# One scan per two channel blocks in a Mamba and mixture-of-experts layer on one core

## The reference, cut to what matters

```python
xc, z = split(layernorm(x) @ in_proj_w.T, 2)
u  = causal_conv(xc, conv_w) + conv_b        # 4 taps, all channels mixed
dt = clip(sigmoid(u @ dt_w.T + dt_b), 1e-4, 1)
A  = -exp(A_log);  B = u @ B_w.T;  C = u @ C_w.T
for each token t:                            # state: 512 channels x 16
    dA    = exp(clip(dt[t] * A, -5, 5))
    state = dA * state + dt[t] * B[t] * u[t] + 1e-6
    y[t]  = sum_n(state * C[t]) + D * u[t]
x = x + (y * silu(z)) @ out_w.T
```

## Time and profile before

| | us |
|---|---|
| median of three runs | 3082.39 |
| profiled execution | 3076.53 |
| its span, first to last instruction | 3074.5 |
| first scan starts | 87.0 |
| first down product of a tile starts | 2418.2 |

### The profile page before, as it was taken

The page is one execution under the profiler, slowest core; times in us unless marked ns, Lnnn a source line. Parts: engine busy times, 40 slices in busy tenths (PEclk is TensorE's granted clock), DMA queues, the critical chain, the costliest instruction groups (busy, mean ns, idle before and its releaser), DMA issues. The chain is left out here.

```text
span 3074.5 us, 57196 instructions
## 1 busy us (share of the span) xinstructions
PE 2651.9 (86%) x15616; PEld 2307.9 (75%) x15616; DVE 2131.7 (69%) x4576; ACT 2115.1 (69%) x4987; POOL 2462.9 (80%) x1667
## 2 busy tenths in 40 slices
PE   6788888898888888988988888889876699999997
PEld 4677877787777777877877777788765577777776
DVE  1889889889888998899899888998894111111111
ACT  1878888888887888888888887888783233333332
POOL 1989999989998999999899988999993365656555
PEclk9889989989988899899898898898987899999999
DMA  3222222223222222222222222222220677777775
GB/s 134 99 70 80 80 73 80 74 75 97 81 77 75 89 73 85 77 74 81 74 79 98 75 76 74 89 74 87 70 70 21 171 184 180 184 177 185 178 184 126
DMA packets 136253, 309.91 MB, mean 101 GB/s; under 512 B 14992, under 2 KB 79632, under 8 KB 135696
## 3 DMA queue, kind: packets, MB, share of 16 engines
q1 hardware_dynamic: 108880, 270.03, 28.0%
q0 software_dynamic: 27072, 36.46, 6.1%
HBM read 258.42 MB, written 48.01 MB: 100 GB/s over the span
## 5 line engine op out<-in xcount | busy, mean ns | idle before, releaser
L1023 POOL TENSOR_TENSOR room<-dtu,b_all 128x1024 f32<-128x1024 f32 x512 | 1202.8, 2368 | 13.3 <-POOL dtu L1000 5.9
L809 ACT ACTIVATE bank<-room,eps_col 128x512 f32<-128x512 f32 x1024 | 693.8, 684 | 309.2 <-DVE carry L1261 213.2
L796 ACT ACTIVATE room<-room,neg_a 128x256 f32<-128x256 f32 x2048 | 868.5, 499 | 9.6 <-DVE room L1247 7.6
L604 PE MATMUL bank<-ident,room 128*128 128x128 f32 x4096 | 556.7, 293 | 239.2 <-DVE room L1256 201.3
L604 PEld LDWEIGHTS bank<-ident,room 128*128 128x128 f32 x4096 | 501.7, 152 | 293.5 <-DVE room L1256 219.5
L1247 DVE TENSOR_TENSOR_SCAN bank<-room,carry,bank 128x256 f32<-128x256 f32 x864 | 580.9, 736 | 61.6 <-ACT bank L809 52.7
L1012 POOL TENSOR_TENSOR room<-room,c_all 128x1024 f32<-128x1024 f32 x224 | 531.8, 2374 | 112.6 <-ACT carry L814 69.2
L1327 DVE SCALAR_TENSOR_TENSOR hid<-hid,bank 128x256 f32<-128x256 f32 (+1 forms) x312 | 131.0, 420 | 631.9 <-ACT up L905 631.9
L1247 DVE TENSOR_TENSOR_SCAN room<-room,carry,bank 128x256 f32<-128x256 f32 x672 | 448.4, 726 | 12.2 <-ACT bank L809 11.5
L1163 POOL DMA_INDIRECT out<-room,ids x144 | 227.7, 1581 | 251.2 <-ACT room L986 221.4
L559 PE MATMUL bank<-xnT,w_conv 128*128 128x256 f32 x3072 | 404.2, 288 | 2.2 <-ACT xnT L832 2.2
(11 more groups left out here) (150 smaller groups left out, 3294.6 us busy)
## 6 DMA issues: line engine op xcount, KB each, us to landing
b_all<-b_scratch SPq DMA_DIRECT2D x128, 512.0 KB, 4.0
c_all<-b_scratch SPq DMA_DIRECT2D x128, 512.0 KB, 5.8
room<-in_wgu SPq DMA_DIRECT2D x72, 704.0 KB, 4.8
room<-in_wd SPq DMA_DIRECT2D x72, 384.0 KB
room<-x_by_expert SPq DMA_DIRECT2D x72, 260.0 KB, 2.7
x_in<-in_x SPq DMA_DIRECT2D x32, 256.0 KB, 5.4
x<-in_x SPq DMA_DIRECT2D x32, 256.0 KB, 2.6
out<-x SPq DMA_DIRECT2D x32, 256.0 KB, 4.2
```

The lines of the kernel that those rows point to most:

```text
L604: last = mm(tr_bank[k][:, b * P:(b + 1) * P], v[n % VRING][:, b, k * P:(k + 1) * P], ident[:, :], is_transpose=True, start=False, stop=(n ...
L796: last = af(da[n % RING][:, b, :], dt[c.par][:, b, :], ACT.Exp, scale=neg_a[:, b, n:n + 1])
L809: af(v_slot(n, h)[:, :], v[n % VRING][:, 2 * h:2 * h + 2, :].rearrange("p b t -> p (b t)"), ACT.Identity, bias=eps_col[:, 0:1]).then_inc(v ...
L1023: nc.gpsimd.tensor_tensor(out=v[n % VRING][:, :, :], in0=dtu[:, :, :], in1=row, op=ALU.mult) \
```

## The change

- The first column of each decay block stays 0 (written once), ScalarE writes columns 1 to 255, and one scan of 512 columns goes over two blocks with the initial value 0.0.
- What the state before brings to a block's first column (decay of the first token x carry) is added to the first column of dt x u x B before ScalarE's addition: `first_args`, `first_decays`, `add_lead`.
- The up half is multiplied by VectorE, from PSUM; ScalarE's copy, the `up` tensor and GpSimd's `hidden` go.
- State 12's product with C goes from GpSimd to VectorE.
- In `start`: raw_x and each tap have a load and a semaphore of their own, the order of loads and of the first chunk's steps changes, w_z is split behind the taps, and VectorE makes the first dt x u.

```diff
-BY_POOL = [0, 2, 4, 6, 8, 10, 12]
+BY_POOL = [0, 2, 4, 6, 8, 10]
...
+        def carried(c):
+            return c.quad * 3 + c.pos - 1
...
-                    load_x(Chunk(0, 0))
+                    sp.dma_start(raw_x, wx).then_inc(x_part_loaded, 16)
+                    for t in range(TAPS):
+                        sp.dma_start(raw_conv[:, :, t, :], wconv[:, :, t, :]).then_inc(tap_loaded[t], 16)
+                        if t == 0:
+                            sp.dma_start(a_raw[:, :, :], a_log).then_inc(w_small, 16)
+                            sp.dma_start(vec[:, 0, :], conv_b).then_inc(w_small, 16)
+                            sp.dma_start(vec[:, 1, :], dt_b).then_inc(w_small, 16)
+                            sp.dma_start(vec[:, 2, :], d_skip).then_inc(w_small, 16)
+                            load_x(Chunk(0, 0))
                     load_x(Chunk(0, 1))
-                    sp.dma_start(raw_x, wx).then_inc(w_raw, 16)
-                    sp.dma_start(raw_conv, wconv).then_inc(w_raw, 16)
...
             def gate_up(c, u, w, xT, tiled):
                 if tiled:
-                    pe.wait_ge(hg_ready, c.index * UNITS + u + HEAD)
-                    pe.wait_ge(up_ready, c.index * UNITS + u + HEAD)
+                    pe.wait_ge(h_ready, c.index * UNITS + u + HEAD)
...
-                    pe.wait_ge(w_raw, 16 * RAW_LOADS)
+                    pe.wait_ge(x_part_loaded, 16)
                     for t in range(TAPS):
+                        pe.wait_ge(tap_loaded[t], 16)
                         for b in range(KM):
+                            n = t * KM + b
+                            if n == TAPS * KM - 1:
+                                pe.wait_ge(pool_const, 11)
+                                pe.wait_ge(comp_done, 2 + 1)
+                                pe.wait_ge(low_done, 2 + 1)
+                                proj_norm(Chunk(0, 0))
...
             def decays(c, n):
                 if n == 0:
-                    act.wait_ge(dt_ready, c.index + 1)
+                    act.wait_ge(dt_ready, c.index * NT + NT)
                 wait(act, half_ready, halves(c, n - RING + 1))
                 for b in range(KD):
-                    last = af(da[n % RING][:, b, :], dt[c.par][:, b, :], ACT.Exp, scale=neg_a[:, b, n:n + 1])
+                    last = af(da[n % RING][:, b, 1:TC], dt[c.par][:, b, 1:TC], ACT.Exp, scale=neg_a[:, b, n:n + 1])
...
             def add_eps(c, n, h):
                 act.wait_ge(v_mul, c.index * NS + n + 1)
+                if c.pos:
+                    act.wait_ge(lead_added, carried(c) * (NS // 2) + n // 2 + 1)
...
+            def first_decays(c):
+                act.wait_ge(first_arg, carried(c) + 1)
+                af(first_da[:, :, :], first_da[:, :, :], ACT.Exp).then_inc(first_da_ready, 1)
...
                 af(hid[0:rows, hid_slot(c, u), :], bank[0:rows, 0:TC], ACT.Tanh, scale=0.5).then_inc(th_ready, 1)
-                act.wait_ge(h_ready, c.index * UNITS + u + HEAD)
-                af(up[0:rows, (c.par + u) % 2, :], bank[0:rows, TC:2 * TC], ACT.Copy).then_inc(up_ready, 1)
...
                     for slot in range(NS):
                         project(Chunk(0, 0), slot)
+                        if slot == 8:
+                            decays(Chunk(0, 0), 0)
+                    add_eps(Chunk(0, 0), 0, 0)
+                    add_eps(Chunk(0, 0), 0, 1)
+                    decays(Chunk(0, 0), 1)
+                    add_eps(Chunk(0, 0), 1, 0)
+                    decays(Chunk(0, 0), 2)
                     take_normed(Chunk(0, 1))
...
                 for h in range(2):
                     dve.wait_ge(v_ready, halves(c, n) + h + 1)
-                    for j in range(2):
-                        b = 2 * h + j
-                        init = carry[:, n, b:b + 1] if c.pos else 0.0
-                        p = v_slot(n, h)[:, j * TC:(j + 1) * TC]
-                        s = v[n % VRING][:, b, :] if n in BY_POOL else p
-                        last = vec_e.tensor_tensor_scan(s, da[n % RING][:, b, :], p, init, ALU.mult, ALU.add)
-                    last.then_inc(half_ready, 1)
+                    decay = da[n % RING][:, 2 * h:2 * h + 2, :].rearrange("p b t -> p (b t)")
+                    p = v_slot(n, h)[:, :]
+                    s = v[n % VRING][:, 2 * h:2 * h + 2, :].rearrange("p b t -> p (b t)") if n in BY_POOL else p
+                    vec_e.tensor_tensor_scan(s, decay, p, 0.0, ALU.mult, ALU.add).then_inc(half_ready, 1)
+
+            def first_args(c):
+                dve.wait_ge(dt_ready, c.index * NT + NT)
+                wait(dve, lead_ready, carried(c) * PIECES)
+                vec_e.tensor_tensor(out=first_da[:, :, :], in0=neg_a_by_state[:, :, :],
+                                    in1=dt[c.par][:, :, 0].unsqueeze(1).to_broadcast([P, NS, KD]), op=ALU.mult) \
+                    .then_inc(first_arg, 1)
+
+            def add_lead(c, n):
+                if n % NEAR == 0:
+                    by_pool, by_dve = kept(c.plus(-1), n + NEAR)
+                    dve.wait_ge(carry_done, by_pool)
+                    dve.wait_ge(dve_kept, by_dve)
+                    dve.wait_ge(first_da_ready, carried(c) + 1)
+                    wait(dve, lead_added, carried(c) * (NS // 2))
+                    vec_e.scalar_tensor_tensor(out=lead_in[:, n:n + NEAR, :], in0=first_da[:, n:n + NEAR, :],
+                                               scalar=CLIP_EXP, in1=carry[:, n:n + NEAR, :], op0=ALU.max,
+                                               op1=ALU.mult).then_inc(lead_ready, 1)
+                    dve.wait_ge(lead_ready, carried(c) * PIECES + n // NEAR + 1)
+                dve.wait_ge(v_mul, c.index * NS + n + 2)
+                firsts = room[:, n % VRING:n % VRING + 2, :, 0]
+                vec_e.tensor_tensor(out=firsts, in0=firsts, in1=lead_in[:, n:n + 2, :], op=ALU.add) \
+                    .then_inc(lead_added, 1)
...
             def gated(c, u, tiled):
                 dve.wait_ge(th_ready, c.index * UNITS + u + 1)
-                dve.wait_ge(up_ready, c.index * UNITS + u + 2 + HEAD)
...
+                dve.wait_ge(hg_ready, c.index * UNITS + u + 1)
+                vec_e.tensor_tensor(out=h, in0=h, in1=gu_bank(c, u, tiled)[0:rows, TC:2 * TC], op=ALU.mult) \
+                    .then_inc(h_ready, 1)
...
                     for h in range(2):
                         proj_dt(Chunk(0, 0), h)
+                        dve.wait_ge(dt_ready, h + 1)
+                        last = vec_e.tensor_tensor(out=dtu[:, 2 * h:2 * h + 2, :], in0=dt[0][:, 2 * h:2 * h + 2, :],
+                                                   in1=uT[0][:, 2 * h:2 * h + 2, :], op=ALU.mult)
+                    last.then_inc(dtu_ready, 1)
...
+                        if scan and slot % 2:
+                            c, n = (scan, slot + 3) if slot + 3 < NS else (proj, slot + 3 - NS)
+                            if c and c.pos:
+                                add_lead(c, n)
+                        if proj and proj.pos and slot == 9:
+                            first_args(proj)
```

More of the change, by code:

```diff
@@ L239, in build @@
         w_early = sem("w_early")
-        w_raw = sem("w_raw")
+        w_small = sem("w_small")
+        x_part_loaded = sem("x_part_loaded")
+        tap_loaded = [sem(f"tap_loaded{t}") for t in range(TAPS)]
         pool_const = sem("pool_const")
@@ L275, in build @@
         carry_done = sem("carry_done")
+        da_zeroed = sem("da_zeroed")
+        first_arg = sem("first_arg")
+        first_da_ready = sem("first_da_ready")
+        lead_ready = sem("lead_ready")
+        lead_added = sem("lead_added")
         tr_ready = sem("tr_ready")
@@ L548, in proj_conv @@
                 if half == 0 and j == 0:
-                    shared = c.plus(-3)
-                    wait(pe, hg_ready, units_out(shared, 1))
-                    wait(pe, up_ready, units_out(shared, 1))
+                    wait(pe, h_ready, units_out(c.plus(-3), 1))
                 if half == 1 and j == 0:
@@ L582, in proj_z @@
                 pe.wait_ge(dt_ready, c.index * NT + k + 1)
+                if c.fixed() and c.index == 0:
+                    pe.wait_ge(comp_done, TAPS * KM + 1)
+                    pe.wait_ge(low_done, TAPS * KM + 1)
                 for n, (b, (x_part, w_part)) in enumerate((b, q) for b in range(KM) for q in PASSES):
@@ L948, in __call__ @@
                             norm_apply(norm)
+                        if proj and proj.pos and slot == 10:
+                            first_decays(proj)
                         if post:
@@ L997, in dt_times_u @@
             def dt_times_u(c):
+                if c.fixed() and c.index == 0:
+                    pool.wait_ge(dtu_ready, 1)
+                    return
                 pool.wait_ge(dt_ready, c.index * 2 + 2)
@@ L1110, in start @@
                         rstd(p_rstd, p_var, p_mv, p_shift, p_var_ready, p_rstd_ready, Chunk(0, n))
+                    pool.wait_ge(comp_done, TAPS * KM + 1)
```

(6 more changed lines are left out.)

77 lines of the change are left out of this document (30 added, 47 removed).

## The result

The changed kernel took **3266.5 us** (3264.6 to 3269.3) where the kernel before took 3083.1: 1.060 times as long, 95% interval 1.058 to 1.062. The forecast was 3039 us, faster; even its slower rival ended at 3117. The change cost 183 us.

What follows compares the result with a forecast made beforehand. No engine full; each loop chunk a TensorE head, then a VectorE tail; tiles wait for GpSimd's product. Start -15, tails +38, heads -14, tiles -48, end -4.5: 3033 us profiled, 5.9 more for the median: 3039 us, range 3006 to 3088.

Steps and rivals of the forecast that it cites:

- the price of the carry's operations on VectorE: Chunk loop, 24 of 32 chunks: 0.1 us per small addition (bounds 0.06 and 0.35), 2.4 us a chunk in sum.
- The rule: Chunk loop: two-SBUF-input VectorE instructions contend with GpSimd, which could lose up to 2 us a chunk; sum would not move.
- the gates: Chunk loop: gate-up product on VectorE makes each of three gates 0.3 us longer, 0.9 us per chunk.
- state 12: Chunk loop's tail: state 12's products and copies on VectorE add 1.3 us per chunk.
- the wide scans: Chunk loop: 512-column scans cost 2.24 us per state instead of 2.57, -0.33; -0.1 in chunks that start a sequence.
- a tail gives back all, a head a quarter: Chunk loop: VectorE work saved in slots 12 to 15 counts fully, in slots 0 to 11 a quarter.
- rival 1: Chunk loop: VectorE's whole work sets it, head and tail count alike; -12 us instead of +24, 3003 us; chance 0.22.
- Tiles: Expert tiles: wait before each down product goes, 8.33 us per tile instead of 9.01; -48 us (bounds -20 and -50).
- Rival 4: Expert tiles stay at 9.0 us because loads, scatters or the gate's signals end last; 3087 us; chance 0.05.
- Start: Up to the first scan: first matmul at 9 us, first convolution near 41, first scan near 69; -15 us.
- End: Last down product ready 2.7 us earlier and likely at full clock, plus -0.5 after the last chunk; -4.5 us.
- Rival 3: TensorE's clock: slow stretch of longer tails grows into heads, 2.5 us a chunk, 78 in all; 3117 us; chance 0.13.

Runs made afterwards that it cites:

- who_waits: Separate test computing nothing of the layer: VectorE operations of each kind, alone and beside GpSimd multiplications; small ones that waited averaged 1.23 us, alone 159 to 170 ns.
- by_reduce: Changed kernel with the carry's small VectorE operations replaced by one-input tensor_reduce in the same places, carry values left out: 3021.7 us.
- old_scan7: Changed kernel with the scans and carry of before (256 columns) and state 12's product back on GpSimd: 2997.3 us.
- pool_late: Changed kernel, carry on GpSimd, its limit on ScalarE, state 12's product back on GpSimd, first_decays behind slot 12's gate: 3012.5 us; 2999.3 without that last move.

## Why the prediction was wrong

- **The failed step is the price of the carry's operations on VectorE.** It took 0.1 us for an addition, bounded it by 0.06 and 0.35, and put 2.4 us to a chunk. The additions held VectorE for 1.09 us, the products for 1.55, all of the carry for 15.4 us a carrying chunk (370 / 24). The bounds came from a row with an input in PSUM and from a drain; no row before had an operation of this kind in the loop, so 0.35 was no bound. Nor did the loop's own upper bound of +80 hold, which rested on it: +261 came. A bound by the nearest rows would have had to ask what an operation of GpSimd lasts: 2.4 us, by the length of L1023 in the earlier trace rows. 8 x 2.4 + 4 x 2.4 = 29 us a chunk was the other end, and 15.4 lies in the middle.
- **The rule was weighed, and charged to the wrong engine.** GpSimd was to lose up to 2 us a chunk, and it had them to spare. But VectorE waited, and in a head it had 4.8 us idle for some 13 us of waiting a chunk (318 / 24). GpSimd's operations are long and it is busy for 43 of a head's 61 us, so 188 of the carry's 312 operations came second. The other order exists too: in who_waits GpSimd's multiplications of 8 columns take 202 ns alone and 572 beside VectorE's additions of 512 columns. The Trainium skill states this for either order, on a page on which the prediction did not draw (SBUF — State Buffer, Who interferes with whom): the two engines share a pair of ports under an exclusive lock, and whichever issues first has it for the whole instruction while the other blocks. By that section a VectorE instruction contends if it has two SBUF inputs, beside a GpSimd instruction that reads SBUF, or if it runs in a two-port mode, as copy and tensor_scalar can; tensor_reduce on trn2 never does. Every line of who_waits agrees.
- **With that one term replaced the sum is right, but in part by luck.** by_reduce has as many small operations as the carry, with its waits and order, and they don't wait for GpSimd. Its loop is 26.4 us over the kernel before (2211.8 - 2185.4); the forecast was 24. The carry's term is right there, 13 us (2211.8 - 2198.8) for 14. Of the others, by the prediction's own steps, the gates were to cost 29 us and cost nothing, state 12 was to cost 42 and cost 59, and the wide scans were to give 61 (35 in tails, 26 in heads) and gave 46. These three errors cancel: 59 - 46 = +13 against 29 + 42 - 61 = +10.
- *Head and tail.* The rule "a tail gives back all, a head a quarter" held as long as TensorE filled the head. At 55.0 us of VectorE work in 60.7 it didn't: the head was VectorE's, and 7.8 us of head came on top of 3.8 of tail. That is rival 1's mechanism, with the opposite sign.
- *Scans*: 1.12 us of pace forecast, 2.24 for two measured, so the pace was right. What it is worth was not: 46 us in the loop with six products and 26 with seven, where 61 were counted. Why less comes through is not shown.
- *State 12 and the gates.* Forecast 42 and 29 us. State 12 cost 59 with the old scans and 39 with the wide ones. The gates cost next to nothing in sum: old_scan7, which has them, the new start and the old scans and products, has the loop of before to a tenth, 2185.4. Its first chunk is 2.9 us shorter (57.2 for 60.1) and the rest as much longer. That ScalarE's and GpSimd's lost work, put at nothing, pays for the gates is a guess; no run parts them.
- *Tiles* -62 for -48: 8.21 us apart, not 8.33, since the down product too got 0.12 shorter (2.59 to the next, 2.71 before). Rival 4 is out.
- *Start* -12.4 for -15, the first matmul at 9.12 for 9 and the first convolution at 41.6 for 40.7. But the first scan came at 74.6, not near 69. State 0's addition is over at 69.25; VectorE's queue has the low part of chunk 1 in front of the scan (L1230 below), and that waited for take_normed, which now stands late in ScalarE's queue. The prediction saw take_normed come late and charged only chunk 1's convolution with it:

```profile
74.01 0.69 DVE L1230 TENSOR_TENSOR xnT<-bank,xnT 128x512 fp32r<-128x512 f32 x1 [5.73 <-ACT xnT L855]
74.62 2.32 DVE L1261 TENSOR_TENSOR_SCAN room<-room,bank 128x512 f32<-128x512 f32 x2
```

- *End*: the last down product waits 1.42 us and takes 2.83 where it waited 4.29 and took 4.52; the wait's part stands in the tiles' stage, and together tiles and end gave 63.4 us for 52.5. The tile that was read, 9.01 us, was also a little under the mean: before, the first 71 down products are 9.06 us apart.
- *Rival 3*: of ten heads of carrying chunks in the changed kernel seven have a granted clock of 0.92 and took 60.6 to 60.8 us. Three have 0.86 and took 60.8, 62.0 and 62.0. So at most some 1.3 us in two heads of ten go with the clock, of 8 us that all grew by. by_reduce has 0.92 or more in the same ten. The clock didn't decide here. In pool_late a lower clock went with the loss of a small gain.

## What to carry to other kernels

Before a small operation is added to VectorE beside a busy GpSimd, look where its operands lie: with two inputs in SBUF, or as a copy or tensor_scalar from SBUF to SBUF, it can cost one whole operation of GpSimd, at times two, however few columns it has. Keep one operand in PSUM (of a copy or tensor_scalar the output will do), use a reduction where one fits, or give the operation to GpSimd's own queue. And price a possible contention on both engines, at the duration of the other one's longest operation, before calling it covered.

## What the runs showed of the hardware

- One wait can span two of GpSimd's operations: 23 of the 76 long products ended with the second, as this one at 1245.1, behind the end of the first at 1242.76 (the longest took 5.06 us):

```profile
1240.39 4.67 POOL L1055 TENSOR_TENSOR room<-dtu,b_all 128x1024 f32<-128x1024 f32 x2
...
1241.83 3.27 DVE L1279 SCALAR_TENSOR_TENSOR lead_in<-first_da,carry 128x16 f32<-128x16 f32 x1
```

- Beside GpSimd's memset VectorE's addition of 8 columns took 160 ns, as alone: this operation of GpSimd, which reads nothing, doesn't hold it.
- A tensor_scalar of 512 columns from SBUF to SBUF takes 422 ns alone against 687 for an addition, so it is in a faster mode. It waits at 8 columns, where it gains nothing (166 ns alone, an addition 161), as at 512 (1231 and 2288 ns beside GpSimd). That the mode is why it waits is what the output in PSUM suggests (163 ns, no wait); no run turns the mode off from SBUF to SBUF.
